# One unit per turn in a chunked delta-rule recurrence, with its loads tied to stages and the gate projections moved behind the others

## The chip, the cores and the metric

The kernel runs on one core of a Trainium2 chip. The metric is the device time of one execution in microseconds, where lower is better. TensorE (PE) multiplies, VectorE (DVE), ScalarE (ACT) and GpSimd (POOL) do element work, and the sync engine (SP) issues most of the DMAs. Each engine executes its own list of instructions in the order in which it is written, and the engines wait for each other through semaphores only.

## The reference, cut to what matters

`x` has 1250 rows of 512. The layer is a graph convolution plus a linear attention on the normalized rows, then a mixture of 4 experts, each a gated delta-rule recurrence over the tokens that were routed to it (2 of 4 per token):

```python
xn = _layernorm(x)
x = x + _L0_gnn_ref(xn, W, b, edge_index) + _L0_mix_ref(xn[None], ...)[0]
x = x + _L0_ffn_ref(_layernorm(x)[None], ...)[0]

# _L0_ffn_ref: 4 experts, top 2, H = 8 heads of 64
q = _l2norm(_silu(h @ Wq)); k = _l2norm(_silu(h @ Wk)); v = _silu(h @ Wv)
def step(S, x):                       # one token, all experts and heads
    S = S * jnp.exp(gt)[..., None, None]
    kv = jnp.einsum('bhk,ebhkv->ebhv', kt, S)
    delta = (vt[None] - kv) * bt[..., None]
    S = S + kt[None, :, :, :, None] * delta[..., None, :]
    ot = jnp.einsum('bhk,ebhkv->ebhv', qt * scale, S)
gate = _silu(h @ Wg)
core = core * rsqrt(mean(core * core)) * o_norm_weight * gate
return core @ Wo
```

## The kernel before, in words

The rows are held in 10 tiles of 125. After the graph convolution and the attention (up to 521 us of the span), three stages follow, and the change touches the first two.

**Projections.** `project_rows(t, w)` (line 744) multiplies tile t by weight w: 0 is queries, 1 keys, 2 values, 3 the output gate. PE runs t from 0 to 9 and w from 0 to 3 inside. ACT applies SiLU to each result (lines 1063 and 1066) and counts it in `f_act`; PE waits for that count before it uses the same PSUM bank again. DVE squares queries and keys (`squares`, line 1657), POOL takes the inverse root (line 1185), DVE scales the rows (`unit_rows`, lines 1665 and 1667) and the gate rows (`gate_rows`, line 1671), and POOL scatters each token's row to the two slots of its experts in the DRAM tensor `qkv_slots` (line 1190). Decays take a similar way: POOL scatters them (line 1180), SP loads them back (line 393), DVE spreads them (`gates_in`, lines 1633 and 1638, behind tile 6), PE sums them behind the last projection (`decay_sums`, lines 764 to 767), ACT exponentiates (`decays`, lines 1046 to 1052), DVE makes rows of them (`decay_rows`), and SP writes these to DRAM and loads them spread over 64 partitions.

**Recurrence.** The 2500 slots are cut into 20 *units* of 128 slots, each of 2 *chunks* of 64. For each unit the inverse of a triangular matrix is built in f16 by four doubling levels and corrected in f32. On PE the stages of a unit are: `features` (line 794, transposes), `key_key`, `key_query` (line 782), `untranspose` (line 813), then `level_m` and `level_t` for levels 1 to 4 (line 782, f16, read from tA and tB), `residual`, `first_fix`, `second_fix` (line 782, f32, read from big). Between them DVE masks or combines each result (for example `level_b`, line 1720) and ACT copies it (`level_up`, lines 1084 and 1086). The chunks carry the state: `old_keys` (line 859), DVE `right_side` (line 1741), `solve` (line 872), ACT `keep_z` (line 1092), `outputs` (lines 883, 893 and 897), DVE `new_state` (line 1748). Line 782 is the line of the helper `products`, 16 products of 64x64 at a time.

The order is written out by hand. Iteration n of 11 builds units 2n and 2n+1 stage by stage (`both`), and puts between these stages the four chunks of the two units before (`chain`). All five engine programs have that loop. SP loads ahead for the next iteration: decay rows (line 404), queries and keys in one DMA per unit (line 420), keys again in another layout in four DMAs of 256-byte pieces (line 411), values (line 416), and it stores the outputs (line 426).

**Output.** POOL gathers the output rows of each token (line 1287), and PE multiplies by `Wo` (line 958).

## Time and profile before

| what | value |
|---|---|
| time, 3 runs | 1128.72 us median (1125.96 to 1130.7) |
| the profiled execution | 1125.21 us, span 1123.3 us |
| mean granted TensorE clock of the span | 0.948 of full |
| PE busy over the span | 962.7 us (86%) |
| DVE, ACT, POOL busy | 598.7, 249.0, 337.2 us |
| projections, first to last matmul | 521.2 to 659.2 us |
| recurrence, first transpose to last new state | 677.7 to 1055.7 us |
| from the last state to the end | 67.6 us |

Line numbers are those of the kernel before. In a row of a timeline the columns are start, duration, engine, line, operation, output and inputs, shapes, the number of instructions merged, and in brackets how long the engine stood idle before it and what ended that. PEld is PE's weight load, which runs beside its matmuls. "issue" is idle time for which the profile has no releaser. An f32 matmul of 64 columns appears as two recorded instructions.

### The profile page before, as it was taken

How to read it: one execution, taken by the hardware profiler on the slowest of the kernel's cores; microseconds unless marked ns; L12 is line 12 of the kernel's file. 1: busy time of each engine (PE TensorE's matmuls, PEld its weight loads, DVE VectorE, ACT ScalarE, POOL GpSimd, SP SyncE). 2: the span in 40 equal slices, each digit the busy share in tenths (PEclk: the TensorE clock that was granted, in tenths of full speed). 3: DMA queues.
4: the chain of work that ended last, by engine and by line, in shares of the span. 5: the costliest groups of instructions: out<-in, count | busy, mean ns of one | idle time of the engine just before them, and what ended most of it. 6: DMA issues, size and time to landing. Idle time of an engine off the chain costs nothing.

```text
span 1123.3 us, 28924 instructions
## 1 busy us (share of the span) xinstructions
PE 962.7 (86%) x12841; PEld 620.7 (55%) x12841; DVE 598.7 (53%) x1297; ACT 249.0 (22%) x497; POOL 337.2 (30%) x284
## 2 busy tenths in 40 slices
PE   0899999999999989988999956878788987888468
PEld 0444444343777734434444426878778877788333
DVE  7878885333777522224533334555555644554265
ACT  0211112100111100003111113324423342233142
POOL 4000000000010000000585346554645464544282
PEclk9899999979999989998999987999999989999879
DMA  9100000000000041000044255443344334422252
GB/s 295 41 1 1 1 1 0 1 0 1 1 1 1 1 157 49 1 0 1 3 171 125 113 206 158 104 108 78 98 113 124 86 86 116 116 68 51 58 159 83
DMA packets 69982, 77.96 MB, mean 69 GB/s; under 512 B 33665, under 2 KB 55323, under 8 KB 69855
## 3 DMA queue, kind: packets, MB, share of 16 engines
q1 hardware_dynamic: 64735, 54.94, 18.1%
q0 software_dynamic: 5120, 21.14, 5.4%
q8 instruction: 103, 1.69, 0.6%
q14 instruction: 24, 0.20, 0.1%
HBM read 51.70 MB, written 24.35 MB: 68 GB/s over the span
## 4 chain that ended last, share of the span: by engine, by line
PE 80%; issue 6%; DVE 6%; ACT 3%; POOL 2%; DMA 1%; SPq 1%; ACTq 0%; DVEq 0%; POOLq 0%
PE bank L782 14%; PE bank L748 12%; PE bank L716 8%; PE bank L489 6%; PE bank L505 4%; PE bank L520 3%; PE bank L958 3%; PE bank L653 3%; PE bank L575 2%; PE bank L883 2%; PE bank L496 2%; PE bank L511 2%; PE bank L872 2%; PE bank L859 2%; PE bank L893 2%
## 5 line engine op out<-in xcount | busy, mean ns | idle before, releaser
L748 PE MATMUL bank<-W,xT 128*128 128x512 f32 x320 | 137.8, 593 | 0.0
L1169 POOL TENSOR_TENSOR big<-big,ident_sb 125x125 f32<-125x125 f32 x10 | 9.9, 989 | 346.2 <-ACT big L1020 346.2
L748 PEld LDWEIGHTS bank<-W,xT 128*128 128x128 f32 x320 | 60.6, 190 | 75.6 <-issue 75.6
L716 PE MATMUL bank<-hs,big 125*125 125x512 f32 x200 | 86.7, 593 | 1.3 <-DVE hs L1547 1.3
L1720 DVE TENSOR_TENSOR tB<-bank,masks_sb 128x512 f16<-128x512 f32 x80 | 52.7, 687 | 59.0 <-PE bank L782 58.8
L489 PE MATMUL bank<-W,xT 128*125 128x512 f32 x160 | 81.8, 610 | 0.0
L1488 DVE TENSOR_SCALAR rows<-iota_sb,tC 128x625 f16<-128x625 f16 x180 | 58.1, 383 | 30.6 <-PE bank L505 30.1
L782 PE MATMUL bank<-tB 64*64 64x64 f16 x2560 | 56.7, 200 | 15.7 <-issue 9.1
L505 PEld LDWEIGHTS bank<-rows 128*125 128x125 f16 x360 | 48.4, 144 | 31.2 <-issue 20.5
L505 PE MATMUL bank<-rows 128*125 128x313 f16 x360 | 62.4, 313 | 2.6 <-DVE rows L1488 2.4
L716 PEld LDWEIGHTS bank<-hs,big 125*125 125x125 f32 x200 | 37.2, 188 | 49.3 <-issue 48.5
L782 PEld LDWEIGHTS bank<-tB 64*64 64x64 f16 x2560 | 52.4, 116 | 19.0 <-issue 16.6
L782 PE MATMUL bank<-big 64*64 64x64 f32 x1920 | 59.1, 219 | 0.0
L782 PEld LDWEIGHTS bank<-big 64*64 64x64 f32 x1920 | 58.1, 135 | 0.3 <-issue 0.3
L1084 ACT ACTIVATE tA<-bank 128x512 f16<-128x512 f32 x60 | 36.0, 600 | 90.4 <-PE bank L782 90.3
L1220 POOL TENSOR_TENSOR big<-state,gtot 128x256 f32<-128x256 f32 x40 | 24.5, 612 | 101.0 <-DVE state L1748 101.0
L782 PE MATMUL bank<-tA 64*64 64x64 f16 x1280 | 34.1, 200 | 23.6 <-issue 20.5
L1398 DVE TENSOR_SCALAR rows<-iota_sb,gbp 125x180 f16<-125x180 f16 x160 | 51.5, 322 | 0.0
L1400 DVE TENSOR_SCALAR rows<-iota_sb,gbp 125x180 f16<-125x180 f16 x160 | 51.3, 321 | 0.0
L1162 POOL TENSOR_TENSOR rstd<-mv,phalf 125x5 f32<-125x5 f32 (+2 forms) x5 | 11.7, 2343 | 128.9 <-DVE mv L1316 128.9
L1227 POOL TENSOR_TENSOR tB<-tA,masks_sb 128x512 f16<-128x512 f16 x20 | 26.7, 1352 | 70.6 <-DVE tA L1705 70.6
L489 PEld LDWEIGHTS bank<-W,xT 128*125 128x125 f32 x160 | 28.0, 191 | 34.1 <-issue 34.1
(286 smaller groups left out, 1902.6 us busy)
## 6 DMA issues: line engine op xcount, KB each, us to landing
big<-qkv_slots SPq DMA_DIRECT2D x20, 512.0 KB, 5.4
rows<-step_rows SPq DMA_DIRECT2D x40, 128.0 KB, 3.8
rows<-gam_rows SPq DMA_DIRECT2D x40, 128.0 KB, 3.3
big<-qkv_slots SPq DMA_DIRECT2D x80, 64.0 KB, 3.9
big<-qkv_slots SPq DMA_DIRECT2D x40, 128.0 KB, 2.8
o_slots<-big SPq DMA_DIRECT2D x40, 128.0 KB, 2.4
x_all<-in_x SPq DMA_DIRECT2D x10, 224.0 KB
out<-tC SPq DMA_DIRECT2D x10, 224.0 KB
```

The source lines that it names most:

```text
L489: last = mm(dst, xT[:, k, t * P:(t + 1) * P], W[:, w, k, :], start=(k == 0 and bias is None), stop=(k == KC - 1))
L505: last = mm(bank[0:P, b0 + k, 0:n], oh_src[:, g % 2, j, 0:P], oh_dst[:, i % WB, t0:t0 + n], start=(j == 0), stop=(j == SC - 1))
L520: last = mm(bank[0:P, b0, :], qs[g % 2][:, c, at:at + P], W[:, 3, c, :], start=False, stop=(c == KC - 1))
L653: last = mm(bank[0:P, 6, :], xT[:, k, s * P:(s + 1) * P], W[:, 4, k, :], start=(k == 0), stop=(k == KC - 1))
L716: last = mm(bank[0:P, t % 2, :], cnt[:, s, t * P:(t + 1) * P], hs[:, s, :], start=(s == 0), stop=(s == NT - 1))
L748: last = mm(bank[:, 2 + w, :], xT[:, k, t * P:t * P + 128], W[:, w, k, :], start=(k == 0), stop=(k == KC - 1))
L782: last = mm(bank[q, b0, a * CL:(a + 1) * CL], lhsT[q, a, :], rhs[q, a, :], start=True, stop=True)
L1084: A(flat(T0[s] if lv == LEVELS - 1 else T16[s]), bank[:, TB[s], :], ACT.Copy).then_inc(S["t_done"], 1)
L1398: V.tensor_scalar(oh_col[:, i % (2 * SB), 0, :], iota[0:P, 0:SW], e_col[:, i:i + 1], e_src[:, i:i + 1], ALU.is_equal, ALU.mult)
L1400: V.tensor_scalar(oh_col[:, i % (2 * SB), 1, :], iota[0:P, 0:SW], e_col[:, i:i + 1], e_dst[:, i:i + 1], ALU.is_equal, ALU.mult).then_inc(S ...
L1488: V.tensor_scalar(oh_dst[:, i % WB, :], iota[:, 0:HN], srt[:, 1, i:i + 1], None, ALU.is_equal).then_inc(S["onehots_done"], 1)
L1720: V.tensor_tensor(B16[s], pm(MB[s]), bm(level[lv], 8), ALU.mult).then_inc(S["b_done"], 1)
```

## The change

It does three things. First, in the recurrence each of the five engine programs takes 22 turns of one unit in place of 11 of two. Turn h starts unit h (up to level 2), finishes unit h-1 (levels 3 and 4 and the corrections), and runs the two chunks of unit h-2. Second, the loads of a unit are issued one unit ahead, each behind a wait for a named stage of the turn, and queries and keys come in two DMAs of half the size. Third, the ten gate projections (w = 3) stand behind all the others, together with their SiLU and their scaling on DVE; `gates_in` moves from tile 6 to tile 7, and the decay sums and exponentials move to tile 8, in the middle of the projections. Everything that is computed stays the same.

```diff
-GAMMA_AT = 6
+GAMMA_AT = 7
+DECAY_AT = 8
...
         def level_count(u, lv):
-            return (LEVELS - 1) * (u - u % 2) + 2 * (lv - 1) + u % 2 + 1
+            return (LEVELS - 1) * u + lv
+        def feature_count(t, w):
+            return 3 * NT + t + 1 if w == 3 else 3 * t + w + 1
+        def feature_bank(t, w):
+            return (5, 2, 3, 4)[t % 4] if w == 3 else 2 + w
...
# SP
-            def load_qk(u):
-                sp.dma_start(qkn[u % 2], qkv_slots[u * SCH:(u + 1) * SCH, 0:2 * D]).then_inc(qk_loaded[u % 2], 16)
+            def load_qk(u, w):
+                sp.dma_start(qkn[u % 2][:, w * D:(w + 1) * D], qkv_slots[u * SCH:(u + 1) * SCH, w * D:(w + 1) * D]).then_inc(qk_loaded[u % 2], 16)
...
-            for n in range(NIT + 1):
-                if n + 1 < NIT:
-                    for s in range(2):
-                        sp.wait_ge(S["eb_done"], 2 * n + s + 1)
-                        load_rows(arow[s], step_rows, 2 * n + 2 + s, arow_loaded[s])
-                    for s in range(2):
-                        sp.wait_ge(S["feat_psum"], 2 * n + s + 1)
-                        load_qk(2 * n + 2 + s)
...
+            for h in range(NSC + 2):
+                if h + 2 < NSC:
+                    sp.wait_ge(S["eb_done"], h + 1)
+                    sp.wait_ge(S["kk_psum"], h + 1)
+                    load_rows(arow[h % 2], step_rows, h + 2, arow_loaded[h % 2])
+                    sp.wait_ge(S["feat_psum"], h + 1)
+                    if h >= 1:
+                        sp.wait_ge(S["t_psum"], level_count(h - 1, 3))
+                    load_qk(h + 2, 1)
+                    sp.wait_ge(S["a_psum"], h + 1)
+                    load_qk(h + 2, 0)
+                if 1 <= h < NSC - 1:
+                    sp.wait_ge(S["kd_done"], h)
+                if h >= 2:
+                    sp.wait_ge(S["o_psum"], 2 * h - 3)
+                load_kp(h + 1, 0)
+                if 1 <= h <= NSC:
+                    sp.wait_ge(S["t_psum"], level_count(h - 1, 4))
+                load_kp(h + 1, 1)
+                if h < NSC:
+                    if h >= 2:
+                        sp.wait_ge(S["y_ready"], 2 * h - 2)
+                    load_vp(h)
+                if h >= 2:
+                    store_o(h - 2)
+                if h + 2 < NSC:
+                    sp.wait_ge(S["qg_done"], h + 1)
+                    load_rows(grow[h % 2], gam_rows, h + 2, grow_loaded[h % 2])
...
# PE, projections
             for t in range(1, NT):
-                for w in range(4):
+                for w in range(1 if t == 1 else 0, 3):
                     project_rows(t, w)
-            decay_sums()
+                if t == DECAY_AT:
+                    decay_sums()
+            pe.wait_ge(W_loaded[3], 32)
+            for t in range(NT):
+                project_rows(t, 3)
...
# PE, recurrence (the lists of ACT, POOL and DVE change in the same way)
+            for h in range(NSC + 2):
+                unit_of(key_key, h)
+                unit_of(level_m, h - 1, 3)
+                chunk_of(old_keys, h, 0)
+                unit_of(key_query, h)
+                unit_of(level_t, h - 1, 3)
+                chunk_of(solve, h, 0)
+                unit_of(untranspose, h)
+                unit_of(level_m, h - 1, 4)
+                chunk_of(outputs, h, 0)
+                unit_of(level_m, h, 1)
+                unit_of(level_t, h - 1, 4)
+                chunk_of(old_keys, h, 1)
+                unit_of(level_t, h, 1)
+                unit_of(residual, h - 1)
+                chunk_of(solve, h, 1)
+                unit_of(level_m, h, 2)
+                unit_of(features, h + 1)
+                unit_of(first_fix, h - 1)
+                chunk_of(outputs, h, 1)
+                unit_of(level_t, h, 2)
+                unit_of(second_fix, h - 1)
...
# DVE
+            for h in range(NSC + 2):
+                unit_of(lower, h)
+                unit_of(level_b, h - 1, 3)
+                chunk_of(right_side, h, 0)
+                unit_of(lower16, h)
+                unit_of(scores, h)
+                unit_of(pairs, h)
+                unit_of(level_b, h - 1, 4)
+                chunk_of(new_state, h, 0)
+                unit_of(level_b, h, 1)
+                chunk_of(right_side, h, 1)
+                unit_of(decay_matrix, h + 1)
+                unit_of(residual, h - 1)
+                unit_of(level_b, h, 2)
+                unit_of(first_fix, h - 1)
+                chunk_of(new_state, h, 1)
+                unit_of(second_fix, h - 1)
```

On PE, the place between the projections and the first transposes of the recurrence. L748 is a projection, L764 to L767 are the decay sums, L794 is `features`. Before:

```order
L748 MATMUL bank<-W,xT 128x512 x144
L764 MATMUL bank<-ident_sb,gbg 128x64 x2
L764 MATMUL bank<-ident_sb,gbg 64x64
L766 MATMUL bank<-gbg,masks_sb 128x320
L767 MATMUL bank<-gbg,masks_sb 128x320
L794 MATMUL bank<-ident_sb,big 128x2x64 x16
L782 MATMUL bank<-big 64x64 x32
```

The same place now (L769 is the projection, L786 to L789 the decay sums, L820 `features`):

```order
L769 MATMUL bank<-W,xT 128x512 x92
L786 MATMUL bank<-ident_sb,gbg 128x64 x2
L786 MATMUL bank<-ident_sb,gbg 64x64
L788 MATMUL bank<-gbg,masks_sb 128x320
L789 MATMUL bank<-gbg,masks_sb 128x320
L769 MATMUL bank<-W,xT 128x512 x52
L820 MATMUL bank<-ident_sb,big 128x2x64 x8
L808 MATMUL bank<-big 64x64 x16
```

The decay sums moved forward by 52 matmuls: the three projections of tile 9 and the ten gate projections, of four each. One unit's transposes follow the projections where two did.

On PE, in the middle of an iteration of the recurrence. L782 with tA is `level_m` or, with tB, `level_t`; L859, L872 and L883 are `old_keys`, `solve` and the first part of `outputs`. Before:

```order
L782 MATMUL bank<-tB 64x64 x64
L859 MATMUL bank<-state,xT 64x64 x8
L782 MATMUL bank<-tA 64x64 x32
L872 MATMUL bank<-tC,W 64x64 x8
L782 MATMUL bank<-tB 64x64 x64
L883 MATMUL bank<-tC,W 64x64 x8
```

The same kind of place now (L808 is `products`, with "big,xT" the `residual` and with "big" alone `first_fix`; L885, L898 and L909 are the chunk's stages, L820 `features`):

```order
L808 MATMUL bank<-tA 64x64 x16
L808 MATMUL bank<-tB 64x64 x32
L885 MATMUL bank<-state,xT 64x64 x8
L808 MATMUL bank<-tB 64x64 x32
L808 MATMUL bank<-big,xT 64x64 x16
L898 MATMUL bank<-tC,W 64x64 x8
L808 MATMUL bank<-tA 64x64 x16
L820 MATMUL bank<-ident_sb,big 128x2x64 x8
L808 MATMUL bank<-big 64x64 x16
L909 MATMUL bank<-tC,W 64x64 x8
```

The f16 stages were 32 and 64 products long and stood together; they are 16 and 32 long now, and f32 stages stand among them.

On SP, the loads of one iteration, from the decay rows on, with what each waits for. Before:

```order
L404 DMA rows<-step_rows 64x2x256 [waits eb_done]
L404 DMA rows<-step_rows 64x2x256
L420 DMA big<-qkv_slots 128x1024 [waits feat_psum] x2
L411 DMA big<-qkv_slots 64x4x64 [waits kd_done]
L411 DMA big<-qkv_slots 64x4x64 x3
L411 DMA big<-qkv_slots 64x4x64 [waits kd_done]
L411 DMA big<-qkv_slots 64x4x64 x3
L416 DMA big<-qkv_slots 64x2x256 [waits y_ready]
```

Now, one turn:

```order
L412 DMA rows<-step_rows 64x2x256 [waits kk_psum,eb_done]
L412 DMA rows<-step_rows 64x2x256
L428 DMA big<-qkv_slots 128x512 [waits t_psum,feat_psum]
L428 DMA big<-qkv_slots 128x512 [waits a_psum]
L419 DMA big<-qkv_slots 64x4x64 [waits o_psum,kd_done]
L419 DMA big<-qkv_slots 64x4x64
L419 DMA big<-qkv_slots 64x4x64 [waits t_psum]
L419 DMA big<-qkv_slots 64x4x64
L424 DMA big<-qkv_slots 64x2x256 [waits y_ready]
L424 DMA big<-qkv_slots 64x2x256
L434 DMA o_slots<-big 64x2x256 [waits o_done]
```

The two loads of queries and keys and the eight of keys stood in a row; they are now one unit's worth at a time, in five places of the turn.

## Rows read from the trace of the kernel before

**Rows 1.** The page: instruction fetches (packets, MB, share), the chain's shares, the projections' group.
```profile
q8 instruction: 103, 1.69, 0.6%
...
PE 80%; issue 6%; DVE 6%; ACT 3%; POOL 2%; DMA 1%; SPq 1%; ACTq 0%; DVEq 0%; POOLq 0%
...
L748 PE MATMUL bank<-W,xT 128*128 128x512 f32 x320 | 137.8, 593 | 0.0
```

**Rows 2.** Stretches of the recurrence: length, busy us (instructions), PE's clock, DMA share, GB/s.
```profile
677.70:709.60 31.90, 26.86 (x800) 24.92 (x802) 16.65 (x24) 12.71 (x24) 17.96 (x15) 0.85 0.62 161
709.60:1041.00 331.40, 274.37 (x9624) 263.33 (x9618) 180.78 (x287) 115.49 (x248) 172.91 (x158) 0.96 0.37 92
1041.00:1056.00 15.00, 10.44 (x304) 9.72 (x304) 3.59 (x9) 2.68 (x7) 1.84 (x3) 1.00 0.10 21
```

**Rows 3.** Who PE waited for, 709.6 to 1041 us: total, times, longest.
```profile
PE bank L782 <- issue: 33.7, 29, 4.2
PE bank L883 <- issue: 7.3, 7, 3.6
PE bank L859 <- issue: 6.5, 8, 1.0
```

**Rows 4.** The timeline from the end of the projections to the recurrence.
```profile
659.17 0.23 PEld L764 LDWEIGHTS bank<-ident_sb,gbg 64*128 64x128 f32 x3 [0.76 <-issue]
...
665.98 0.95 POOL L1190 DMA_INDIRECT qkv_slots<-big,posi  x1 [0.30 <-issue]
...
673.00 1.01 SPq L420 DMA_DIRECT2D big<-qkv_slots  x2
...
677.72 3.59 PE L794 MATMUL bank<-ident_sb,big 128*128 128x128 f32 x16 [16.89 <-DMA big<-qkv_slots]
```

**Rows 5.** Stretches from one restart of PE to its next, columns as in rows 2.
```profile
876.35:880.33 3.98, 2.85 (x127) 2.73 (x126) 1.12 (x2) 2.45 (x5) 1.78 (x3) 1.00 0.54 110
723.33:727.22 3.89, 2.94 (x126) 2.70 (x126) 1.62 (x3) 2.73 (x6) 2.46 (x2) 1.00 0.02 4
727.23:731.43 4.20, 2.85 (x127) 2.73 (x126) 1.12 (x2) 2.45 (x5) 2.02 (x3) 1.00 0.52 129
1029.60:1033.21 3.61, 2.91 (x125) 2.80 (x126) 1.02 (x2) 2.34 (x5) 0.83 (x1) 1.00 0.15 41
863.50:868.69 5.19, 3.12 (x130) 2.92 (x126) 2.61 (x6) 1.09 (x2) 5.19 (x6) 0.98 0.68 195
```

**Rows 6.** DVE's timeline of `gates_in` and one tile's squares and scaling.
```profile
630.17 0.39 DVE L1633 COPY gbg<-gbp 128x160 f32<-128x160 f32 x2
...
639.36 1.23 DVE L1657 TENSOR_TENSOR tB<-big 128x1024 f32<-128x1024 f32 x1 [8.05 <-issue]
...
642.56 0.71 DVE L1667 TENSOR_TENSOR big<-big,nrm 128x512 f32<-128x512 f32 x1
```

**Rows 7.** PE's and SP's timeline in the iteration from 858 us.
```profile
859.73 2.03 PE L782 MATMUL bank<-xT,big 64*64 64x64 f32 x64
...
862.25 6.22 SPq L411 DMA_DIRECT2D big<-qkv_slots  x8
...
872.90 1.18 PE L782 MATMUL bank<-tB 64*64 64x64 f16 x64
...
874.40 0.41 PE L782 MATMUL bank<-tA 64*64 64x64 f16 x16
...
885.78 1.97 PE L794 MATMUL bank<-ident_sb,big 128*128 128x128 f32 x16
```

**Rows 8.** Groups by line and shape, 709.6 to 1041 us: busy, mean ns, idle before.
```profile
L1720 DVE TENSOR_TENSOR tB<-bank,masks_sb 128x512 f16<-128x512 f32 x72 | 47.4, 687 | 52.6 <-PE bank L782 52.5
...
L1084 ACT ACTIVATE tA<-bank 128x512 f16<-128x512 f32 x54 | 32.4, 600 | 81.0 <-PE bank L782 81.0
```

**Rows 9.** DVE's timeline in the last four chunks, which run alone.
```profile
1040.89 0.41 DVE L1741 TENSOR_TENSOR tC<-big,bank 128x256 f32<-128x256 f32 x1
...
1044.84 0.42 DVE L1741 TENSOR_TENSOR tC<-big,bank 128x256 f32<-128x256 f32 x1 [1.04 <-PE bank L859]
```

More of the change, by code:

```diff
@@ L744, in project_rows @@
             def project_rows(t, w):
-                if t:
-                    pe.wait_ge(S["f_act"], 4 * (t - 1) + w + 1)
+                b0 = feature_bank(t, w)
+                if w < 3 and t:
+                    pe.wait_ge(S["f_act"], feature_count(t - 1, w))
+                if w == 3 and 1 <= t < 4:
+                    pe.wait_ge(S["f_act"], feature_count(NT - 1, t - 1))
+                if w == 3 and t >= 4:
+                    pe.wait_ge(S["f_act"], feature_count(t - 4, 3))
                 for k in range(KC):
-                    last = mm(bank[:, 2 + w, :], xT[:, k, t * P:t * P + 128], W[:, w, k, :], start=(k == 0), stop=(k == KC - 1))
+                    last = mm(bank[:, b0, :], xT[:, k, t * P:t * P + 128], W[:, w, k, :], start=(k == 0), stop=(k == KC - 1))
                 last.then_inc(S["f_psum"], 1)
-            for w in range(4):
+            for w in range(3):
                 pe.wait_ge(W_loaded[w], 32)
                 project_rows(0, w)
+            project_rows(1, 0)
             pe.wait_ge(S["gate_step"], 1)
```

222 lines of the change are left out of this document (77 added, 145 removed).

## The prediction, made before the result was known

> **What bounds the kernel now.** I read the chain of waits first: 80% of it is PE, and 6% is "issue", time for which no releaser is seen [rows 1]. So the change pays through PE's idle time. The timeline by engine shows two kinds of it in the changed stages.
>
> The first is a single hole. PE is done with the decay sums at 677.72 - 16.89 = 660.83 us and starts the first transposes at 677.72 [rows 4]. In it the last tile's rows are scattered (last issue 665.98), and the loads of queries and keys start at 673.00 [rows 4].
>
> The second is spread over the recurrence. The stretches say 331.4 us for nine iterations of two units, with 274.4 us of PE busy [rows 2]: 18.41 us for one unit and its two chunks, 15.24 of them busy. Of the 57 us idle, 33.7 + 7.3 + 6.5 = 47.5 us are "issue" [rows 3], not a wait for DVE or ACT. These restarts fall in the middle of stages, and from one to the next PE runs 125 to 127 matmuls and as many weight loads, about 253 instructions with what is not recorded beside them [rows 5]. The queue of instruction fetches moves 1.69 MB in 103 packets, 16.4 KB each [rows 1]. I read this as PE waiting for the next block of its own instructions. Four blocks with a restart at both ends took 3.98, 3.89, 4.20 and 3.61 us, 3.92 in the mean, with 2.85 to 2.94 us of work in each [rows 5]. One that met SP's burst of eight loads (issued from 862.25 [rows 7]), at a DMA share of 0.68, took 5.19 us [rows 5].
>
> **The change, part by part.**
>
> *Gate projections behind the others.* A projection costs 137.8 / 40 = 3.44 us [rows 1]. None is added or removed. Ten of them, 34.4 us, now stand between the last value projection and the first transposes. Before, the way from the last value projection to the first transposes held one gate projection, the decay sums (1.7 us) and the hole, about 3.4 + 0.8 + 1.7 + 16.9 = 22.8 us. That is under 34.4, so scatter, decay rows and first loads are hidden with some 11 us to spare. What is left of the hole is the wait for the last SiLU, which also counts in `f_act`: two hops of 0.2 us and 0.60 us of ACT [rows 8], 1.0 us. If the cover were gone the 16.9 us would be back.
>
> *Decay sums at tile 8.* PE reaches them right behind the value projection of tile 8. `gates_in` on DVE stands behind the squares of tile 8 and the scaling of tile 7. From the end of the key projection to the start of the squares are 0.2 + 0.6 us and a hop; from there (639.36) to the end of the scaling (642.56 + 0.71) 3.9 us, and the copies 0.4 [rows 6]: 5.4 us, while PE has 3.44 us of work. PE waits 2.0 us where it waited 0.76 [rows 4], so +1.2. ACT loads its table for the exponentials and back for SiLU, some 5 us in all against 10.3 us between two uses of a bank; that is hidden. A hole of 2 us can cost a stretch at the lower of PE's two clock levels, which the trace does not show here. Bounds: 0 and 1.7 us (one extra half of a projection's 3.44). I take 1.2. The first transposes then stand at 660.8 + 2.4 + 1.0 = 664.2, a gain of 13.5 us.
>
> *`gate_rows` on DVE.* Ten times 0.68 us now lies under the gate projections, which leave DVE free; only the last one stands before `lower(0)`, beside 1 us of transposes and 1 us of `key_key`. Cost nothing; if the cover failed, 0.7 us.
>
> *One unit per turn: fill and drain.* Before, the fill took 31.9 us for two units [rows 2]. Now turn 0 is one unit alone through level 2. Its chain is transposes 1.0, copy 0.6, `key_key` 1.0, DVE 0.69 + 0.65, `untranspose` 0.4, DVE 0.65, two levels of 0.4 + 0.69 + 0.7 + 0.6, the next transposes, and a dozen hops of 0.2: 13.5 us. Turn 1 has 10 us of PE work and level chains beside it, 12.5 us by the same steps. Sum 26, a gain of 5.9. The drain was 15 us by the stretch to 1056 and 14.7 to the last state at 1055.7 [rows 2]; a chunk alone takes 1044.84 - 1040.89 = 3.95 us [rows 9]. Turn 20 now finishes unit 19 beside two chunks (its chain from level 3 to `second_fix`, 10.6 us plus what the chunks put between), 12 us, and turn 21 is two chunks alone, 8 us: 20, a loss of 5.3.
>
> *One unit per turn: the 18 full turns.* I laid the 21 stages of a turn one behind another, from half of the two-unit groups (f32 stage 2.03 / 2, `level_t` 1.18 / 2 and its tail, `level_m` 0.41, transposes 1.97 / 2 [rows 7]), with DVE 0.69 and ACT 0.60 per stage [rows 8] in their own new orders and 0.2 us per hop. (The hop is from a chunk alone: 3.95 us with 2.7 us of work and six hops.) The operands come before PE gets there at nearly every stage, because each of the two units has only two levels in a turn. The thinnest places are `level_t` 3 (mask ready at 2.8, PE there at 3.0), `level_m` 4 (4.3 against 4.6), and `outputs` of the first chunk, whose ACT copy stands behind both copies of level 3 and comes 0.3 us late. A turn comes out at 16.0 us. So semaphores do not bound it; the fetch does. One unit with its chunks is 536 matmuls, 4.24 blocks of 126.5, and at 3.92 us each that is 16.6 us. Before, f16 stretches ran through a block in 2.9 us and waited while f32 stretches, near 3.8 us a block, gave nothing back; the new order mixes the two, so the wait approaches that floor. I add 0.7 us for blocks that meet a load: the burst cost an iteration up to 2 us, and it is now halved and in five places, but it comes each turn. 17.3 us a turn: 18 x (18.41 - 17.3) = 20.0 us gained. Bounds: 16.0 (no fetch wait) and 22.0 (every block like the one of 5.19 us).
>
> *Loads.* Queries and keys in two DMAs adds 20 issues on SP, at about 0.5 us each (673.00: two in 1.01 [rows 4]). SP has 14 issues a turn, some 9 us of 17, and each load is needed most of a turn later; the spread is the only effect, and it is in the 0.7.
>
> *After the recurrence* nothing moves except one gate scaling on DVE that was not on the path.
>
> Sum: 13.5 + 5.9 - 5.3 + 20.0 = 34.1 us. From the profiled execution's 1125.2 us that gives 1091.1, its span 1123.3 - 34.1 = 1089.2. That execution lay 3.5 us under the median of 1128.7, from which the same step gives 1094.6. I take 1093.
>
> **A rule weighed.** The restarts of rows 5 bear on fetching. The Trainium skill, "Runtime: NRT & Kernel Launch", section "Instruction fetch mechanics", says the instruction store is refilled in blocks of 256 instructions while the current one runs, and that this is hidden. Of the block's length the trace agrees (127 + 126 recorded); that it is hidden the trace does not bear out, if I read the "issue" rows rightly. By that rule there is no floor of 16.6 us, which is the second rival below.
>
> **The rivals.**
>
> *The turn stays at 18.4.* The fetch takes as long as it did and the new order only moves the waits. For it: a block took 3.89 us at a DMA share of 0.02 and 3.98 at 0.54 [rows 5], so thinner loads hardly make it faster. Against: the mixing. Gain 14.1: 1113 us.
>
> *No fetch floor.* The "issue" waits come from the old order itself and go with it; the turn takes the 16.0 us of the walk. For it: PE has no other wait. Against: restarts in the middle of a stage, at equal counts of instructions. 18 x 1.3 = 23 us more: 1070 us.
>
> *Loads all over the turn, the slow one.* Before, one or two blocks of 8.5 per iteration met the burst. If now three of four blocks meet a load and take 5.19 us [rows 5], a block is 4.87 us and the turn 20.7: 18 x 2.25 = 40 us lost against 14.1 gained, 1155 us. It decides from a turn of 18.41 + 14.1 / 18 = 19.2 us, or 4.53 us a block, which is half of the blocks. Against: the block at a share of 0.54 took 3.98 us [rows 5]; only the burst did harm.
>
> *The hole stays.* Something in the way to the first loads does not move forward (decay rows, the last scatter) and PE waits as before: 13.5 us less, 1107 us. Against: it would need over 11 us more than the trace shows.
>
> **How the numbers follow.** Forecast 0.70, turn stays 0.12, no floor 0.08, hole stays 0.05, slow 0.05. The forecast's own spread is a turn of 16.8 to 18.0, so 1084 to 1106. The range 1079 to 1115 takes in the turn that stays and part of the no-floor case, and leaves out the slow one. About 0.5% (5.6 us) is what a measurement of this kernel can tell from no change. The slow rival gives slower 0.05; between it and the turn that stays lies same, 0.04; faster 0.91.
>
> **What would show it.** Right: PE idle before the first `features` about 1 us, and these at about 664 us; PE idle about 2 us before the decay sums; a turn of about 17.3 us, counted from one `second_fix` to the next; "issue" still the largest releaser, but in shorter pieces, about 1.5 to 2 us a turn, and PE's clock nearer to full over the recurrence; a drain of 20 us. Wrong: ACT or DVE as releasers of more than 1 us a turn would mean that the walk missed a wait; a turn at 16 would mean the fetch was no floor; blocks above 4.5 us would mean that the loads found the fetch.

## The result and the profile after

The kernel after takes 1089.96 us, the median of four runs (1087.67 to 1092.03); the kernel before took 1127.34 us beside it (four runs, 1125.81 to 1130.7). The ratio is 0.9664, with a 95% interval from 0.9631 to 0.9697: 3.4% less time. The profiled execution took 1091.14 us, its span is 1089.1 us.

The lines of the page that answer to [rows 1], first the busy time of each engine:

```profile
PE 951.0 (87%) x12841; PEld 610.3 (56%) x12841; DVE 593.7 (55%) x1297; ACT 254.5 (23%) x498; POOL 331.4 (30%) x284
...
q8 instruction: 103, 1.69, 0.7%
...
PE 82%; DVE 7%; issue 6%; POOL 2%; ACT 2%; DMA 0%; SPq 0%; DVEq 0%; POOLq 0%
...
L769 PE MATMUL bank<-W,xT 128*128 128x512 f32 x320 | 138.0, 593 | 0.0
```

PE issues the same 12841 matmuls and as many weight loads from the same 103 blocks of instructions, and a projection costs what it did. The idle time between them is less, and so is the busy time (951.0 us against 962.7), at a mean granted clock of the span of 0.965 instead of 0.948.

The timeline around the decay sums and before the first transposes (start, duration, engine, line; in brackets the wait before it and its releaser), to be laid beside [rows 4]:

```profile
613.37 0.39 DVE L1652 COPY gbg<-gbp 128x160 f32<-128x160 f32 x2
613.81 0.39 PE L786 MATMUL bank<-ident_sb,gbg 64*128 64x64 f32 x3 [1.48 <-DVE gbg L1652]
...
660.14 0.60 ACT L1094 ACTIVATE hs<-bank 125x512 f32<-125x512 f32 x1 [2.84 <-PE bank L769]
660.80 1.09 PE L820 MATMUL bank<-ident_sb,big 128*128 128x128 f32 x8 [0.69 <-ACT hs L1094]
```

The hole of 16.89 us is gone. PE waits 1.48 us before the decay sums, for `gates_in` on DVE, and 0.69 us before the first transposes, for the last SiLU.

The stretches of the recurrence, cut as in [rows 2] (columns as there): the fill, the 18 full turns from one `second_fix` to the one 18 units later, the drain.

```profile
660.80:685.90 25.10, 19.69 (x604) 17.64 (x606) 14.06 (x20) 9.56 (x18) 18.64 (x15) 0.93 0.44 129
685.12:1000.65 315.53, 267.88 (x9655) 256.41 (x9651) 174.66 (x287) 121.00 (x250) 165.12 (x159) 0.99 0.38 101
1001.30:1020.40 19.10, 14.86 (x462) 13.60 (x462) 6.14 (x14) 4.64 (x11) 1.84 (x3) 1.00 0.10 20
```

For the before kernel the same cut (`second_fix` of unit 0 at 707.96, of unit 18 at 1039.34) gives:

```profile
707.96:1039.34 331.38, 274.64 (x9640) 263.74 (x9636) 180.76 (x287) 115.49 (x248) 172.91 (x158) 0.96 0.37 93
```

The same matmuls (9640 and 9655 recorded) stand in 315.5 us instead of 331.4, a turn of 17.53 us instead of 18.41. PE's busy time fell with its idle time, from 274.6 to 267.9 us, at a granted clock of 0.99 instead of 0.96. Over all the span is 34.2 us shorter; stage by stage (us, from the start of the one event to the start of the next):

| stage | before | after | gain | predicted |
|---|---|---|---|---|
| start to the first projection (code not changed) | 521.2 | 518.9 | 2.3 | 0 |
| to the first `features` | 156.5 | 141.9 | 14.6 | 13.5 |
| to `second_fix` of unit 0 | 30.3 | 24.3 | 6.0 | 5.9 |
| 18 turns | 331.4 | 315.5 | 15.9 | 20.0 |
| to the last state | 15.9 | 19.7 | -3.8 | -5.3 |
| to the end | 68.1 | 68.8 | -0.7 | 0 |

Measured as the prediction did it, the fill went from 31.9 to 25.1 us and the drain from 14.7 to 19.5, a gain of 6.8 and a loss of 4.8.

Who PE waited for in the 18 turns (total us, times, longest), the answer to [rows 3]:

```profile
PE bank L808 <- issue: 26.6, 33, 2.0
PE bank L885 <- issue: 6.6, 6, 1.5
PE bank L839 <- issue: 4.9, 4, 1.6
PE bank L919 <- issue: 4.5, 4, 1.4
PE bank L909 <- ACT tC L1119: 2.3, 8, 0.3
PE bank L909 <- issue: 1.7, 3, 1.3
```

"issue" is 44.3 us in all. It was 47.5. What changed is its shape: no piece is longer than 2.0 us, where there were pieces of 4.2 and 3.6. ACT holds PE for 2.3 us over 18 turns, before the first part of `outputs`. Before, waits for ACT were 6.3 us in that stretch:

```profile
PE bank L782 <- ACT big L1086: 2.9, 2, 1.7
PE bank L883 <- ACT tC L1092: 2.6, 5, 0.7
PE bank L782 <- ACT tA L1084: 0.8, 5, 0.2
```

PE's restarts inside a stage are still there, and two stretches from one to the next answer to [rows 5]. The timeline, then the stretches:

```profile
852.72 0.66 PE L808 MATMUL bank<-tB 64*64 64x64 f16 x29 [1.59 <-issue]
...
856.93 0.43 PE L808 MATMUL bank<-tA 64*64 64x64 f16 x15 [1.12 <-issue]
...
869.57 0.21 PE L919 MATMUL bank<-state,W 64*64 64x64 f32 x1 [0.89 <-issue]
```

```profile
852.72:856.93 4.21, 3.08 (x126) 2.95 (x127) 2.13 (x3) 2.47 (x5) 1.31 (x2) 1.00 0.30 72
869.57:873.12 3.55, 2.91 (x126) 2.83 (x126) 2.25 (x3) 2.53 (x5) 0.94 (x1) 1.00 0.12 26
```

Again 126 or 127 of each, and 3.55 to 4.21 us.

### The profile page after: what moved, and what is told of

It reads as the page before. It is cut to its first block, busy times and chain, and to the rows that moved or that the text cites. A ratio compares the mean times of both kernels' runs of the same rounds, so it can differ in the third digit from the quotient of the medians.

```text
span 1089.1 us, 29006 instructions
## 1 busy us (share of the span) xinstructions
PE 951.0 (87%) x12841; PEld 610.3 (56%) x12841; DVE 593.7 (55%) x1297; ACT 254.5 (23%) x498; POOL 331.4 (30%) x284
## 4 chain that ended last, share of the span: by engine, by line
PE 82%; DVE 7%; issue 6%; POOL 2%; ACT 2%; DMA 0%; SPq 0%; DVEq 0%; POOLq 0%
PE bank L808 15%; PE bank L769 12%; PE bank L732 8%; PE bank L505 6%; PE bank L521 4%; PE bank L536 3%; PE bank L977 3%; PE bank L669 3%; PE bank L591 3%; PE bank L512 2%; PE bank L909 2%; PE bank L820 2%; PE bank L527 2%; PE bank L885 2%; PE bank L919 2%
## 5 line engine op out<-in xcount | busy, mean ns | idle before, releaser
L769 PE MATMUL bank<-W,xT 128*128 128x512 f32 x320 | 138.0, 593 | 0.0
L769 PEld LDWEIGHTS bank<-W,xT 128*128 128x128 f32 x320 | 60.6, 190 | 75.3 <-issue 75.1
L808 PE MATMUL bank<-tB 64*64 64x64 f16 x2560 | 58.8, 193 | 18.4 <-issue 16.2
L808 PE MATMUL bank<-big 64*64 64x64 f32 x1920 | 67.9, 220 | 4.7 <-issue 3.0
L808 PEld LDWEIGHTS bank<-big 64*64 64x64 f32 x1920 | 61.0, 135 | 10.0 <-issue 8.4
L808 PEld LDWEIGHTS bank<-tB 64*64 64x64 f16 x2560 | 51.4, 110 | 20.7 <-issue 20.7
L1249 POOL TENSOR_TENSOR tB<-tA,masks_sb 128x512 f16<-128x512 f16 x20 | 23.3, 1166 | 102.4 <-DVE tA L1722 102.4
L994 ACT ACTIVATE xT<-bank 128x500 f32<-128x500 f32 x20 | 11.3, 589 | 146.3 <-PE bank L497 146.3
L919 PE MATMUL bank<-state,W 64*64 64x64 f32 x640 | 40.6, 218 | 4.5 <-issue 4.5
```

What stands on the lines that cost most here:

```text
L769: last = mm(bank[:, b0, :], xT[:, k, t * P:t * P + 128], W[:, w, k, :], start=(k == 0), stop=(k == KC - 1))
L808: last = mm(bank[q, b0, a * CL:(a + 1) * CL], lhsT[q, a, :], rhs[q, a, :], start=True, stop=True)
L919: mm(bank[q, DB, o0 + j * DH:o0 + (j + 1) * DH], qG[u // 2 % 2][u % 2][q, c2 * HB + j, :], state[q, c % 2, j, :], start=True, stop=False)
```

## Experiments

The questions were three. Are the two halves of the change worth what the prediction says, each alone? Is the floor of a turn a count of instructions, as the prediction has it, or work and waits? And what do the loads and their pacing do to it? Medians are given with their runs; each ratio is to the kernel before, run on the same chip, with its 95% interval.

### The two halves, each alone

`e1_gates_only` is the kernel before with the new order of the projections:

```diff
-            for w in range(4):
+            for w in range(3):
                 pe.wait_ge(W_loaded[w], 32)
                 project_rows(0, w)
...
-            decay_sums()
+                if t == DECAY_AT:
+                    decay_sums()
+            pe.wait_ge(W_loaded[3], 32)
+            for t in range(NT):
+                project_rows(t, 3)
```

> The kernel before, with only the projection part of the change: gate projections behind the others, their scaling on DVE with them, decay sums at tile 8. Theory (the hole before the recurrence closes by itself): PE's hole of 16.9 us becomes about 1 us, 1.5 us goes to the wait before the decay sums, and the first products no longer run at the lower clock: 14 to 16 us faster, about 1112 us. Rival (the hole only moves, because the first loads are late for two units at once): under 5 us faster, 1123 us or more.

`e2_turns_only` is the kernel after with the projections in their old order (the same edit the other way round).

> The changed kernel with the projection part put back as it was before: only the recurrence in turns of one unit and its loads behind stages. Theory: 6.8 us from the fill, 16.0 from the 18 full turns, less 4.8 in the drain, so 17 to 19 us faster than before, about 1109 us; together with the projections alone it adds up to the whole (0.966 times before). Rival (the two parts need each other, since the new fill depends on loads that are long there): under 12 us faster.

Measured: 1110.45 us (1107.93 to 1113.24), ratio 0.9835 (0.9788 to 0.9882), for the projections alone; 1113.24 us (1110.2 to 1114.06), ratio 0.9854 (0.9809 to 0.9899), for the turns alone. Against 1127.64 us of before that is 17.2 and 14.4 us, 31.6 together. The whole change gave 37.4 us at first, and 31.0 us when it was run again (below), so the halves add up within what the medians can tell. The first half gained somewhat more than its 14 to 16 us, the second less than its 17 to 19, and both rivals (under 5, under 12) are out by the medians. The first two windows are of `e1`: from its first `features` to `second_fix` of unit 0, then the 18 units.

```profile
664.10:691.57 27.47, 22.88 (x744) 21.37 (x746) 16.06 (x24) 12.49 (x24) 17.94 (x15) 0.94 0.47 144
691.57:1024.95 333.38, 275.92 (x9640) 264.25 (x9636) 180.89 (x286) 115.49 (x248) 172.93 (x158) 0.96 0.38 93
```

The fill before, cut in the same way:

```profile
677.70:707.96 30.26, 25.22 (x744) 23.28 (x746) 15.27 (x22) 12.71 (x24) 17.96 (x15) 0.84 0.59 158
```

The same two of `e2`:

```profile
681.30:708.22 26.92, 22.42 (x576) 20.40 (x578) 13.67 (x19) 9.56 (x18) 17.67 (x15) 0.76 0.47 126
708.22:1023.69 315.47, 269.40 (x9655) 258.11 (x9651) 174.63 (x288) 121.04 (x250) 164.99 (x160) 0.99 0.39 102
```

In `e1` the way from the first projection to the first `features` is 141.9 us, 14.6 less than before, and the turns take 333.4 us, no less than the 331.4 of before. In `e2` that way is 157.0 us and the turns take 315.5. Each half is worth its own stage, with one exchange. After the hole the granted clock of the fill is low (0.76 in `e2`). Without it the fill is 2.8 us shorter at the same work (30.3 before, 27.5 in `e1`), and of the two kernels with turns of one unit the one with the hole has a fill longer by 2.6 us (26.9 in `e2`, 24.3 after). The profiled execution of `e1` does not show more than that: 14.6 and 2.8 us gained, 2.0 us lost in turns whose code is that of before. So 18 turns of the same code can differ by 2 us between two kernels, and a smaller difference is not read as the worth of an edit below.

### Is it a count of instructions?

In one place of each turn, `untranspose`, PE gets work that is thrown away. `e6_one_wide` adds one product of 128x512 in f32, which the trace shows as two matmuls (1.13 us together) and two weight loads; `e7_three_wide` adds three of them; `e8_many_small` computes the stage's sixteen f16 products three times, 64 more instructions a turn for very little work.

```diff
...
+                for i in range(1):        # 3 in e7
+                    mm(bank[:, MB[s], :], ident[:, :], W[:, 4, i % KC, :], start=True, stop=True)
                 for a in range(8):
```

```diff
-                for a in range(8):
-                    for b in range(2):
+                for i in range(3):        # e8
+                    for a in range(8):
+                        for b in range(2):
```

> The changed kernel with one f32 matmul of 512 columns more per unit, ahead of untranspose, into the bank that untranspose then overwrites: 0.86 us of PE work in 4 instructions, 20 times, 17 us of work. Theory (PE waits for its instruction blocks, about 2.5 us a turn, and work that needs no instructions fills that wait): 0 to 7 us slower than the changed kernel. Rival (no floor, PE's work is what bounds): 15 to 18 us slower.

> The same with three such matmuls per unit: 2.6 us of PE work in 12 instructions, 52 us in all. Theory: the wait of about 2.5 us a turn is used up and the rest shows, 15 to 35 us slower than the changed kernel. Rival (no floor): 48 to 54 us slower.

> The changed kernel with the sixteen f16 products of untranspose issued three times in place of once (the same values into the same bank): 32 matmuls and 32 weight loads more per unit, at 25 ns a pair 0.8 us of PE work, about as much as one wide matmul, but 64 instructions in place of 4. Theory: a quarter of a block of 3.9 us more per unit, 1.0 us, 17 to 21 us slower than the changed kernel, and far from the one wide matmul. Rival (no floor): about the same as the one wide matmul, 14 to 17 us slower both.

Measured: `e6` 1096.99 us (1094.6 to 1099.89), ratio 0.973 (0.9686 to 0.9773); `e7` 1112.28 us (1108.23 to 1113.4), 0.9856 (0.9811 to 0.99); `e8` 1108.78 us (1107.13 to 1110.28), 0.9829 (0.9788 to 0.9869). The 18 turns, of `e6`:

```profile
692.99:1007.23 314.24, 284.96 (x9692) 260.34 (x9687) 174.15 (x287) 120.80 (x250) 165.05 (x159) 1.00 0.39 101
```

of `e7`:

```profile
689.71:1021.67 331.96, 313.09 (x9764) 272.64 (x9759) 175.04 (x288) 120.93 (x250) 164.93 (x160) 1.00 0.37 96
```

and of `e8`:

```profile
690.78:1019.43 328.65, 274.14 (x10231) 263.62 (x10227) 175.10 (x288) 120.42 (x250) 165.14 (x160) 0.99 0.38 97
```

Read the first two numbers of each row against 315.53 and 267.88. `e6` does 17.1 us more work in a time that is no longer (1.3 us less, inside the 2 us above): the work fell into the restarts, and "issue" went from 44.3 to 28.8 us. `e7` does 45.2 us more work and the turns grow by 16.4, with 18.5 us of "issue" left. `e8` does 6.3 us more work, and the turns grow by 13.1, with "issue" at 54.4 us. Work in few instructions is free until it has used up the idle time; instructions cost even where they hardly work. Against the 1089.96 us of the kernel after, the medians are 7.0, 22.3 and 18.8 us higher, within what was expected of each (for `e6` at its edge), but part of that lies outside the 18 turns, in the first stages and in the fill. The largest waits of `e8`:

```profile
PE bank L808 <- issue: 28.4, 33, 1.7
PE bank L910 <- issue: 16.0, 9, 2.1
PE bank L840 <- issue: 10.0, 9, 1.6
```

The queue of instruction fetches says that these are blocks of PE's code. It moved 103 packets in both kernels. On `e8`'s page:

```profile
PE 962.9 (87%) x13481; PEld 620.6 (56%) x13481; DVE 595.8 (54%) x1297; ACT 254.0 (23%) x498; POOL 328.9 (30%) x284
...
q8 instruction: 108, 1.77, 0.7%
```

640 more matmuls and 640 more loads (13481 - 12841 each) are 1280 instructions, 5.1 blocks of 253, and there are 5 packets more. In the 18 turns they are 1152 instructions, 4.6 blocks; 13.1 us over them is 2.9 us a block, where a quarter of 3.9 us a unit had been expected. That is less than the mean block of the turns, which is (9655 + 9651) / 253 = 76.3 blocks in 315.5 us, 4.13 us each. So the count is not all that sets a block's time; it was 4.35 us before, 4.30 in `e7` and 4.06 in `e8`.

### What the loads do to it

`e5_no_loads` brings nothing in from unit 2 on:

```diff
-                if h + 2 < NSC:
+                if h + 2 < 0:
                     sp.wait_ge(S["eb_done"], h + 1)
...
-                pe.wait_ge(qk_loaded[u % 2], 32 * (u // 2 + 1))
+                pe.wait_ge(qk_loaded[u % 2], 32)
```

> The changed kernel without the loads of units 2 to 19 in the recurrence: every unit reads what units 0 and 1 left in the buffers, so the outputs are not the reference's; PE, DVE, ACT and POOL run the same instructions, and the stores stay. Theory (an instruction block has a least time of about 3.6 to 3.9 us without any load): the turn falls from 17.5 to 16.6 to 17.0 us, restarts in the middle of stages every 126 to 127 matmuls stay, 10 to 17 us faster than the changed kernel. Rival (the waits are collisions of fetches with loads): they go, and the turn falls to the 16.0 us of the semaphore walk or less, 27 us faster.

Measured: 1071.46 us (two runs, 1070.37 and 1072.56), ratio 0.95 (0.9451 to 0.955). The 18 turns, and one block among them:

```profile
686.54:981.95 295.41, 264.71 (x9654) 254.41 (x9651) 174.51 (x287) 120.78 (x250) 165.91 (x161) 1.00 0.09 20
...
856.09:859.91 3.82, 2.91 (x126) 2.83 (x126) 2.25 (x3) 2.53 (x5) 1.69 (x3) 1.00 0.02 4
```

Its waits of PE in the turns:

```profile
PE bank L798 <- issue: 17.7, 25, 1.2
```

The turn is 16.4 us, 3.87 us a block. "issue" fell from 44.3 to 27.6 us but did not go, and the block above took 3.82 us at a DMA share of 0.02. So there are two parts. One is a floor under a block that stays when the loads are left out (the stores remain, a DMA share of 0.09). The other is what all the loads together add, 20.1 us over 18 turns, 1.1 us a turn. That is more than the theory's 10 to 17 us. The rival is out, since the restarts did not go, though the turn came near its 16.0 us.

Two kernels change how the loads come. `e3_loads_unpaced` takes the change's waits on stages out and keeps those that guard a buffer:

```diff
-                    sp.wait_ge(S["kk_psum"], h + 1)
                     load_rows(arow[h % 2], step_rows, h + 2, arow_loaded[h % 2])
...
-                    sp.wait_ge(S["a_psum"], h + 1)
                     load_qk(h + 2, 0)
...
-                if 1 <= h <= NSC:
-                    sp.wait_ge(S["t_psum"], level_count(h - 1, 4))
                 load_kp(h + 1, 1)
```

`e4_qk_one_load` brings queries and keys in one load:

```diff
-                    load_qk(h + 2, 1)
-                    sp.wait_ge(S["a_psum"], h + 1)
-                    load_qk(h + 2, 0)
+                    load_qk(h + 2)
```

> The changed kernel without the five waits in SP's list that only place a load behind a stage of the turn (key_key, level_t 3, untranspose, outputs, level_t 4); the waits that protect a buffer stay. Theory (instruction blocks take about 3.9 us each, and only a burst of loads makes them longer): loads bunch up again, but with one unit's worth; 3 to 9 us slower than the changed kernel. Rival 1 (the turns' gain comes from the placing): the turn goes back to 18.4 us, 16 us slower. Rival 2 (the placing is worth nothing): within 2 us.

> The changed kernel with queries and keys of a unit in one DMA of 512 KB again, issued behind level_t 3; the wait for untranspose goes with the second DMA. Theory: rows of 4 KB in place of two of 2 KB move the same bytes with half the packets, within 2 us of the changed kernel. Rival (one long load holds an instruction block up): 4 to 8 us slower.

Measured: `e3` 1103.51 us (1093.91 to 1106.6), ratio 0.9762 (0.9693 to 0.9832); `e4` 1105.12 us (1102.34 to 1108.05), 0.9782 (0.9736 to 0.9828). The turns of `e3`:

```profile
690.83:1010.79 319.96, 267.20 (x9655) 256.73 (x9651) 174.49 (x288) 120.89 (x250) 164.67 (x159) 0.99 0.38 99
```

of `e4`:

```profile
695.42:1015.67 320.25, 270.24 (x9655) 259.08 (x9651) 174.83 (x287) 121.04 (x250) 164.89 (x159) 0.98 0.38 99
```

Each loses 4.4 to 4.7 us in the turns, a quarter of a microsecond a turn. For `e3` that is the theory; for `e4` the theory (within 2 us) is out and its rival holds. In `e3` all of it is idle time of PE; in `e4` half is busy time (270.2 us against 267.9, at a clock of 0.98). In the times they stand 13.5 and 15.2 us above 1089.96. I had read these two differences of the medians as the worth of the edits; they are not. In the two profiled executions 3.5 and 7.6 us of the difference already stand where none of the edits reaches: the first projection starts at 518.9 us in the kernel after, at 522.4 in `e3` and at 526.5 in `e4`. Another 2.3 and 2.8 us stand in the fill (26.6 and 27.1 us against 24.3), at a granted clock of 0.87 instead of 0.93. The loads of the fill are edited too, but `e8` has that clock there without such an edit, so this part can't be put down to the loads. So the kernel after was run again.

### The same kernel again, and the decay sums one tile later

`e9_changed_again` is the kernel after, with no edit. `e10_decay_sums_later` moves the decay sums behind tile 9:

```diff
-DECAY_AT = 8
+DECAY_AT = 9
```

> The changed kernel once more, beside the next two and the kernel before on one chip, because its 18 turns were 4.4 and 4.7 us shorter in the traces than those of the two kernels with other loads, while the times lay 13.5 and 15 us apart: 3.5 and 7.6 us of that already stood at the first projection, in code that none of them changes. If that part wanders from execution to execution (TensorE's clock rises at another moment in the first 60 us), the time here is anywhere from 1088 to 1098 us, and the 18 turns are 315 to 316 us again. If it belongs to the program, 1090 us and a first projection at 519 us again.

> The changed kernel with the decay sums behind tile 9 in place of tile 8. The wait of 1.5 us for DVE's copies goes, since these are then 10 us old; the way from the decay sums to the first loads is about 17 us and still lies under the ten gate projections of 34 us. Theory: first projection to first transposes 140.4 us in place of 141.9, and 1 to 2 us faster than the changed kernel beside it, if that can be seen at all. Rival (the decay rows are now too late): a wait for DMA before the first transposes, slower.

Measured: `e9` 1093.55 us (five runs, 1088.65 to 1095.8), ratio 0.9716 (0.969 to 0.9742); `e10` 1091.43 us (five runs, 1089.29 to 1095.1), 0.97 (0.968 to 0.9719). The turns of `e9`, then of `e10`:

```profile
689.87:1005.32 315.45, 267.59 (x9655) 256.37 (x9651) 174.77 (x287) 120.86 (x250) 164.89 (x159) 0.99 0.39 101
```

```profile
691.37:1005.56 314.19, 269.18 (x9654) 257.95 (x9651) 174.55 (x288) 121.03 (x250) 164.93 (x159) 0.99 0.39 101
```

The stages of `e9` from the first projection to the last turn are those of the kernel after to 0.1 us (way to `features` 141.8, turns 315.45), but its first projection starts at 523.7 us, 4.8 us later, with the same code ahead of it. The median of the same kernel moved by 3.6 us. In `e10` the wait before the decay sums is gone, and the way to `features` is 140.3 us, 1.6 less. The medians differ by 2.1 us, and the two ratios' intervals overlap over most of their width: the trace shows a gain on the way, the times do not tell it from none. The turns of `e10`, whose code was not touched, are 1.3 us shorter than those of `e9`. It is the best version found, if there is a difference at all.

### Which loads?

`e11_no_key_rows` leaves out the key rows from unit 2 on, 256 KB a unit in pieces of 256 bytes; `e12_no_query_key_loads` leaves out queries and keys, 512 KB a unit. The first lets each packet count, the second each byte.

```diff
-                load_kp(h + 1, 0)
...
-                load_kp(h + 1, 1)
+                if h < 1:
+                    for c in range(2):
+                        load_kp(1, c)
```

```diff
-                    load_qk(h + 2, 1)
-                    sp.wait_ge(S["a_psum"], h + 1)
-                    load_qk(h + 2, 0)
```

> The changed kernel without the loads of the keys in their second layout for units 2 to 19 (closing_keys reads what units 0 and 1 left, so the outputs are not the reference's). They are 256 KB of a unit's 1.3 MB of loads, but 1024 packets of 256 bytes of its some 2300. Leaving out all loads shortened the 18 turns by 20.1 us. Theory A (a load holds instruction blocks up by its packets): about 9 us of these go, the turns take 306 to 308 us. Theory B (by its bytes): about 4 us, 311 to 312 us.

> The changed kernel without the loads of queries and keys that the transposes read, for units 2 to 19 (they transpose what units 0 and 1 left, so the outputs are not the reference's). These are 512 KB of a unit's 1.5 MB. Leaving out all loads shortened the 18 turns by 20.1 us, leaving out the key rows in 256-byte packets (256 KB) by 2.0. Theory (these two halves fall into the f16 part of the turn, where PE uses up its instruction blocks fastest, and so cost most): 8 to 14 us less, the turns take 301 to 307 us. Rival (the cost goes by bytes, 2 to 3.4 us per 256 KB): 4 to 7 us less, 308 to 311 us.

Measured: `e11` 1087.84 us (1084.84 to 1092.06), ratio 0.9662 (0.9639 to 0.9686); `e12` 1089.77 us (1087.06 to 1093.54), 0.9672 (0.9609 to 0.9735). The turns of `e11`, then of `e12`:

```profile
687.49:1001.03 313.54, 270.95 (x9655) 260.95 (x9651) 174.85 (x287) 120.73 (x250) 164.83 (x160) 0.97 0.32 88
```

```profile
689.61:1000.57 310.96, 267.43 (x9655) 256.14 (x9651) 174.72 (x287) 120.89 (x250) 165.49 (x161) 0.99 0.31 76
```

Against 315.5 us the turns are 2.0 us shorter without the key rows and 4.5 us shorter without queries and keys. The reading by bytes, made for `e12`, fits, and both that were made for `e11` were too high. By packets the small pieces would have cost more than the large ones. But `e11` is a weak witness: turns of the same code differed by 2.0 us between `e1` and before, and by 1.3 us between `e10` and `e9`, so its 2.0 us are not told from none. Its granted clock was 0.97 and its busy time 3.1 us above that of the kernel after, so that its idle time fell by 5.1 us, against 4.1 in `e12`. That the cost follows bytes is not shown. Together these two loads are 768 KB of a unit's 1.57 MB of loads (the 1.3 MB of the expectation was too low), and 6.5 us of the 20.1 that all loads cost; the rest was not divided.

### What the packets of the instruction queue show

The traces keep the start and the length of every packet, those of the instruction queue too (16 KB each, one for each block). I lay them beside PE's restarts, taken as idle time of over 0.35 us in the turns. In the kernel after there are 38 such restarts, and every one comes 1.20 to 1.62 us after the end of a packet of this queue. In `e5` it is 33 of 33, at 1.23 to 1.61 us. Before it is 37 of 41, and the profile puts the other four down to ACT. So PE's restarts in these turns follow the arrival of code. For the blocks with a restart at both ends, mean us of each part:

| kernel (blocks) | restart to start of packet (longest) | packet | end of packet to restart | whole |
|---|---|---|---|---|
| before (17) | 1.80 (4.68) | 1.07 | 1.41 | 4.28 |
| after (20) | 1.65 (2.91) | 1.11 | 1.41 | 4.17 |
| `e9`, the same kernel (25) | 1.72 (2.84) | 1.07 | 1.42 | 4.21 |
| `e3_loads_unpaced` (22) | 1.81 (2.91) | 1.16 | 1.46 | 4.43 |
| `e4_qk_one_load` (24) | 1.82 (3.57) | 1.07 | 1.38 | 4.26 |
| `e5_no_loads` (13) | 1.40 (1.47) | 1.16 | 1.39 | 3.94 |

The floor is this chain: the next packet starts 1.4 us after PE has restarted, takes 1.1 us, and PE goes on 1.4 us after its end. The loads do not lengthen the packet; they put off its start. In the block of 5.19 us of [rows 5], which met SP's burst, the packet started at 866.00 us, 5.4 us after the one before it, and took 1.39 us. The first part is longer in `e3` and `e4` than in the two traces of the kernel after, as their turns are, but by little more than these two differ.

## Why the prediction came out right, and where it did not

The forecast was 1093 us; 1089.96 us was measured, and 1093.55 us when run again. The whole was right, and all its parts but one within 1.5 us. That the profiled execution's 34.2 us meet the forecast's 34.1 so closely is in part luck: the turns brought 4.1 us less, the way to `features` 1.1 and the fill and drain 1.6 us more than forecast, and 1.6 us come from stages whose code did not change.

**The hole.** Right. The forecast put the first `features` at 664.2 us; they start at 660.8 here. With the start of the first projection taken out, which moved by 2.3 us on its own, that is a gain of 14.6 us against 13.5. The wait before the decay sums was 1.48 us, not 2.0, and the one before `features` 0.69, not 1.0. The rival "the hole stays" is out: `e1` alone takes the hole away. Of the 2.4 us that the forecast's sum adds ahead of `features`, 1.2 are the longer wait, where 0.7 was measured. The other 1.2 can only be the clock that a wait of 2 us might cost. The granted clock stayed at 1.00 from the decay sums to the first `features`, so this term was nothing, and without it the forecast would have been 14.7 us.

**Fill and drain.** The gain of 6.0 us (5.9 forecast) and the loss of 3.8 (5.3) are near, by laying stages one behind another; cut as the prediction cut them they are 6.8 and 4.8. The walk gave the new fill 26 us, and it took 25.1. But what the 5.9 us consist of was not seen. The walk took the prices of stages from the turns, and what it was taken from, the 31.9 us of before, had run at a granted clock of 0.85 [rows 2] behind the hole. So the gain holds the clock's part, which no term of the prediction names: 2.8 us by `e1`. One unit per turn is worth only 3.2 us there, as the 24.3 us of the kernel after against the 27.5 of `e1` say.

**The turn.** This is the term that was mis-sized: 15.9 us against 20.0, a turn of 17.53 us against 17.3, still inside the forecast's 16.8 to 18.0. Its mechanism stood: a block of some 253 instructions has a shortest time, and semaphores do not bound the turn. `e6` and `e8` show it from both sides, and they rule out "no fetch floor", which would have had `e6` grow by 17.1 us; it did not grow. `e5` shows which half of the sum was off. Without loads the turn is 16.4 us, against the forecast's floor of 16.6; the loads add 1.1 us, against 0.7. Two more things were off. The first was "the new order mixes the two, so the wait approaches that floor" of 3.92 us a block. In the whole 18 turns the fetch waits fell by only 3.2 us, from 47.5 to 44.3, which is 2.5 us a turn and not the forecast's 1.5 to 2, and the mean block is 4.13 us. The second was what the gain consists of. As an account, the 15.9 us are 6.8 of busy time, as the granted clock went from 0.96 to 0.99; 4.0 of waits for ACT, 6.3 before and 2.3 after; 3.2 of fetch waits; and 1.9 of idle time that no wait names. As causes they can't be read off so, since `e6` showed that work goes in and out of the restarts without moving the end. What the runs show as a cause is how the loads stand in the turn: about 4.4 us come back with the pacing taken out (`e3`) and about 4.7 with queries and keys in one load (`e4`). The two are not to be added, since each puts the same loads closer together. The prediction gave nothing to that, and everything to the mixing of stages. What the mixing is worth was not tested: no run has the old order with its loads spread, or without loads.

The clock's part can be read from the trace of before. Its turns have six stretches at the lower of PE's two levels (1.2 and 2.4 GHz), and each begins within 1.2 us of the end of one of PE's stalls of 1.95, 2.82, 3.09, 3.61, 3.64 and 4.19 us. No stall outside these six is longer than 1.72 us. After the change there is one such stretch, behind a stall of 1.87 us, and none behind the longest, of 2.04 us. So the 6.8 us of busy time go with the end of the long stalls.

One reading of [rows 5] was wrong: the stretch of 5.19 us does not begin at a restart. PE does not stop at 863.50 us, and the stretch holds 130 matmuls. It ends at one, after 1.95 us of idle time.

**The fetch.** The Trainium skill, "Runtime: NRT & Kernel Launch", section "Instruction fetch mechanics", gives as the reason why fetching is hidden that the engine issues more slowly than blocks come in. The traces here do not agree for this stretch. With 17.1 us more work in the same blocks (`e6`) the turns took no longer, and the restarts come 1.20 to 1.62 us after the end of a packet of code. In this recurrence PE is done with its instructions before the next block is there, and the fetch is not hidden. Even in `e7`, with 313.1 of 332.0 us busy, 18.5 us of "issue" are left.

**Loads.** The slow rival, blocks of 5.19 us all over the turn, is out. It was right that loads lengthen blocks: 0.7 us a turn was set aside for that, and 1.1 us was measured, 295.4 against 315.5 us over 18 turns. It was wrong that the spread over a turn is the only effect of the two halves of queries and keys and that it costs or gives nothing of its own: `e3` and `e4` lose 4.4 and 4.7 us in the turns. This rests on one trace of each. The turns of the unedited kernel agree to 0.1 us between its two, but those of untouched turn code in other kernels lie up to 2.0 us apart.

**The rival "the turn stays at 18.4"** would have been 1113 us. Its argument, that a thinner load hardly makes a block faster, has some right: without any load a block is 3.87 us, and it took 3.89 us at a share of 0.02 in [rows 5]. The mean of the blocks moved, by 0.22 us, and not the fastest.

**Left open.** What the 1.4 us before a packet of code and the 1.4 us behind it consist of. What the mixing of stages is worth by itself. How the cost of the loads divides beyond the two that were left out, and whether it goes by bytes.

## What to carry to other kernels

Where a stretch of small matmuls shows PE restarting after an equal count of instructions, with "issue" as the releaser, count instructions and not work. Here 17.1 us of work in a few wide products were free, until the idle time was used up, and 6.3 us of work in 1152 small instructions cost 13.1 us. Lay the packets of the instruction queue beside the restarts to see whether it is the code that PE waits for. Spread loads over such a stretch: bunched loads cost 4.4 and 4.7 us in 18 turns here. Sum a change by stages from the trace, and run the unedited kernel again before reading differences of some microseconds between medians as the worth of an edit.

## What was not expected of the hardware

Two executions of the same code reached the first projection 518.9 and 523.7 us after their start. PE's clock differed in the first stages. The stretch from 20 to 60 us (length, PE busy, granted clock, DMA share, GB/s) of the kernel after:

```profile
20.00:60.00 40.00, 28.33 (x94) 0.91 0.30 105
```

and of the same kernel in `e9`:

```profile
20.00:60.00 40.00, 28.89 (x80) 0.83 0.30 107
```

and of `e1`, whose code up to there is the same too:

```profile
20.00:60.00 40.00, 29.35 (x89) 0.96 0.31 109
```

The granted clock of one early stretch thus differs by up to 0.13 between executions, and the first projection starts anywhere between 518.8 and 526.5 us in the fourteen traces. Why is open: `e1` has the highest clock there and starts its first projection at 522.2 us, later than the kernel after, so this stretch alone does not explain it.

A block of PE's instructions took 3.87 us in the mean with the loads left out, 15 ns for each of its 253 instructions, where PE had 3.47 us of work in the mean block and 2.91 us in the one shown above, which took 3.82. That a stretch of small f16 and f32 products is bounded there, and not by its matmuls, I had read from restarts only; that 17.1 us of work could be added for nothing I had not expected in full. Nor had I expected that the loads put off the start of a packet of code and leave its length as it is.
